# Two-layer transformer on one core: the middle stage's last batch written tile by tile, with banks and key buffers of its own

## The reference, cut to what matters

```
attn   = softmax(q k^T / 4) v                      # 16 heads of 16
out    = (sigmoid(gate) * mem_out / denom + (1 - sigmoid(gate)) * attn) @ Wo.T
x      = out + experts of layer 0 ; xn = layernorm(x)
q1, k1 = silu(xn @ Wq1), silu(xn @ Wk1) ; v1 = silu(xn @ Wv1)
sg     = sigmoid((xn @ Wg1) @ Wg2)                 # Wg1: 256 x 16
logits = xn @ router1                              # 256 x 8, top 2, softmax over the two
```

## Time and profile before

| what | us |
|---|---|
| median of 3 runs | 997.73 (994.32 to 1004.47) |
| the profiled execution | 995.28 |
| its span in the profile | 993.4 |
| busy: TensorE, VectorE, ScalarE, GpSimd | 837.8, 573.7, 394.2, 311.4 |
| middle stage's last outT copied | 567.31 |
| first transfer of the next stage | 635.38 |

### The profile page before, as it was taken

The page is one execution under the profiler, slowest core; times in us unless marked ns, Lnnn a source line. Parts: engine busy times, 40 slices in busy tenths (PEclk is TensorE's granted clock), DMA queues, the critical chain, the costliest instruction groups (busy, mean ns, idle before and its releaser), DMA issues. The chain is left out here.

```text
span 993.4 us, 14867 instructions
## 1 busy us (share of the span) xinstructions
PE 837.8 (84%) x4544; PEld 486.6 (49%) x4544; DVE 573.7 (58%) x1269; ACT 394.2 (40%) x676; POOL 311.4 (31%) x250
## 2 busy tenths in 40 slices
PE   4989999848998987997988748399799999999990
PEld 4765655501223443433434436256566666666660
DVE  7746877258779776777674435424343443444435
ACT  2336666414555565466446604022122222222220
POOL 3033567363001330151015113214243344344230
PEclk9999999956999997999798966599899999999995
DMA  8514655463222323533403301799773344344007
GB/s 273 136 59 146 198 184 183 151 187 92 86 67 61 117 85 100 170 106 107 145 27 107 127 21 61 213 288 307 209 171 99 92 125 115 90 116 124 23 16 259
DMA packets 158353, 130.26 MB, mean 131 GB/s; under 512 B 64128, under 2 KB 139920, under 8 KB 158288
## 3 DMA queue, kind: packets, MB, share of 16 engines
q1 hardware_dynamic: 151136, 109.89, 37.6%
q0 software_dynamic: 7152, 19.54, 6.7%
HBM read 83.37 MB, written 46.01 MB: 130 GB/s over the span
## 5 line engine op out<-in xcount | busy, mean ns | idle before, releaser
L1305 DVE TENSOR_REDUCE b_negmax<-b_psM 128x1 f32<-128x512 f32 x256 | 163.0, 683 | 61.0 <-PE b_psM L1491 58.2
L1242 ACT ACTIVATE b_probs<-b_psE 128x512 f32<-128x512 f32 x256 | 138.8, 594 | 125.9 <-PE b_psE L1509 125.1
L1491 PE MATMUL b_psM<-b_kst,b_qst 96*128 96x512 bf16 x256 | 98.5, 427 | 42.1 <-DVE b_negmax L1305 26.0
L1509 PE MATMUL b_psE<-b_qst,b_kst 98*128 98x512 bf16 x256 | 87.9, 405 | 14.1 <-ACT b_probs L1242 9.6
L2007 PE MATMUL d_psG<-d_w,d_xT 128*128 x156 | 76.9, 616 | 2.5 <-issue 1.4
L1860 POOL DMA_INDIRECT scratch_ys<-d_y,put x39 | 39.7, 1018 | 122.4 <-ACT d_y L1891 120.8
L2032 PE MATMUL d_psY<-d_w,d_hidden 128*128 x312 | 76.8, 390 | 0.8 <-ACT d_hidden L1885 0.8
L2015 PE MATMUL d_psU<-d_w,d_xT 128*128 x156 | 75.0, 603 | 0.0
L1491 PEld LDWEIGHTS b_psM<-b_kst,b_qst 96*128 96x128 bf16 x256 | 24.5, 99 | 101.4 <-DVE b_negmax L1305 76.7
L1518 PE MATMUL b_psV<-b_probs,b_vst 128*32 128x512 f32 x512 | 71.9, 634 | 2.5 <-ACT b_probs L1242 2.5
L1509 PEld LDWEIGHTS b_psE<-b_qst,b_kst 98*128 98x128 bf16 x256 | 20.4, 98 | 101.0 <-issue 51.8
(11 more groups left out here) (353 smaller groups left out, 1591.0 us busy)
## 6 DMA issues: line engine op xcount, KB each, us to landing
scratch_parts<-a_parts SPq DMA_DIRECT2D x12, 512.0 KB, 4.2
b_qst<-scratch_parts SPq DMA_DIRECT2D x96, 64.0 KB, 2.1
b_kst<-scratch_parts SPq DMA_DIRECT2D x96, 64.0 KB, 2.1
scratch_parts<-b_part SPq DMA_DIRECT2D x24, 256.0 KB, 3.1
d_qst<-scratch_parts SPq DMA_DIRECT2D x96, 64.0 KB
d_kst<-scratch_parts SPq DMA_DIRECT2D x96, 64.0 KB
scratch_ys<-a_y SPq DMA_DIRECT2D x39, 128.0 KB, 1.8
scratch_v<-a_xn SPq DMA_DIRECT2D x4, 1024.0 KB, 6.9
```

Source lines behind the costliest of these rows:

```text
L1242: nc.scalar.activation(probs[k % PSLOTS][:, h, :], psE[h % 2][:, :], ACT.Exp, scale=float(HD) ** -0.5).then_inc(scores_used[h % 2], 1)
L1305: nc.vector.tensor_reduce(negmax[i][:, t, h:h + 1], psM[:, h % 2, :], AX_X, ALU.max, negate=True).then_inc(rows_used[h % 2], 1)
L1491: nc.tensor.matmul(psM[:, h % 2, :], qst[g][0:STACK, h, t * P:(t + 1) * P], kst[g][0:STACK, h, :], start=True, stop=True).then_inc(rows_re ...
L1509: nc.tensor.matmul(psE[h % 2][:, :], kst[g][0:STACKM, h, k * P:(k + 1) * P], qst[g][0:STACKM, h, :], start=True, stop=True).then_inc(score ...
```

## The change

For the last batch the shared steps are replaced by a function `finish` on each engine.

- The V projection of the third batch is no longer in slot 15 of the fourth batch's attention; it comes in `finish`, behind the output projection.
- Heads, turn and output projection, residual, moments, the turn of xn and its split go by tile, in psM, psV and the banks of the scores (psS, the old psE in one tensor).
- The last batch's k has buffers of its own (half1, parts1, in the memory of probs). Its parts are made by ScalarE and GpSimd; the last one was made on VectorE.
- The order on TensorE is: small projection, q with the logits' turn between its halves, k, rank, turn of k, V, gate, inversion.
- On VectorE the tables follow the choice at once, the decayed k comes behind the ids, the weights of the two experts come last. The gate and the exponential of the weights are last on ScalarE.

For all batches the small projection is made with its result turned: the weights (24 columns) stand still and the 512 rows pass, in 6 products. VectorE copies the 24 x 512 result (lowT), and four small products with the identity turn logits and gate input (24 columns for each tile). The choice of experts moves from slot 10 to 11, its exponential on ScalarE from 11 to 12, and its weights from 12 to 13.

TensorE's order between the last scores and the norm, before. psV<-b_probs is `values`, b_outT and b_qf are the heads, b_combined the turn, b_wo the output projection; the rows b_wv ahead are the end of the 24 of V.

The three instructions on b_part are gone from VectorE, and the decayed k stands behind the ids. The diff, cut to its core:

```diff
-            for slot in sorted(steps):
...
+            finish(BATCHES - 1)
+
+        def final(b, g, k):
+            return isinstance(b, int) and b == BATCHES - 1 and g == GROUPS - 1 and k == TILES - 1
+
+        half1 = probs[1][:, 0:KT, :]
+        parts1 = [probs[0][:, j, :].bitcast(BF16).rearrange("p (k t) -> p k t", k=KT) for j in range(3)]
+        turned = [psM[:, 0, 0:KT * P], psM[:, 1, 0:KT * P], psS[:, 0, 0:KT * P], psS[:, 1, 0:KT * P]]
+        projected = [psV[:, 0:D], psM[:, 0, 0:D], psV[:, 0:D], psS[:, 0, 0:D]]
...
+            def finish(n):
+                store(n - 1)
+                store_xn(n)
+                sp.wait_ge(qd_done, n + 1)
+                sp.dma_start(scratch["qd"][n].rearrange("k p n -> p k n"), qd[:, :, :]).then_inc(stored, 16)
+                store_parts(n, 0, parts)
+                sp.wait_ge(kd_done, n + 1)
+                sp.dma_start(scratch["kd"][n].rearrange("(t p) n -> p t n", p=P), kd[:, :, :]).then_inc(stored, 16)
+                sp.wait_ge(v_done, n + 1)
+                sp.dma_start(scratch["v1"][n].rearrange("(t p) n -> p t n", p=P),
+                             v32[:, :, :, :].rearrange("p t h w -> p t (h w)")).then_inc(stored, 16)
+                store_parts(n, 1, parts1)
+                store_gate(n)
...
+            def finish(n):
+                for t in range(TILES):
+                    combine(t)(n)
+                power(n)
+                decay_q(n)
+                rest(0)(n)
+                third(n)
+                pool.wait_ge(part_done[0], 2 * n + 2)
+                pool.wait_ge(k_ps, n + 1)
+                nc.gpsimd.tensor_tensor(half1, half1, parts1[0], ALU.subtract).then_inc(rest_done, 1)
+                pool.wait_ge(part_done[1], 2 * n + 2)
+                nc.gpsimd.tensor_tensor(parts1[2], half1, parts1[1], ALU.subtract).then_inc(part_done[2], 1)
...
+            def finish(n):
+                for t in range(TILES):
+                    act.wait_ge(combT_ps, n + t + 1)
+                    nc.scalar.activation(combT[:, :, t * P:(t + 1) * P], psX[:, t % 2, 0:KT * P].rearrange("p (k n) -> p k n", k=KT),
+                                         ACT.Copy).then_inc(combT_done, 1)
+                silu_v(n - 1)
+                for t in range(TILES):
+                    act.wait_ge(xT_ps, n + t + 1)
...
+                silu_half(0)(n)
+                first_part(n)
+                act.wait_ge(half_ps, 2 * n + 2)
+                nc.scalar.activation(half1, psM[:, :, :], ACT.Silu).then_inc(half_done, 1)
+                second_part(n)
+                act.wait_ge(half_done, 2 * n + 2)
+                nc.scalar.activation(parts1[0], half1, ACT.Copy).then_inc(part_done[0], 1)
+                act.wait_ge(v_ps, n + 1)
+                act.wait_ge(stored, STORES * n)
+                nc.scalar.activation(v32[:, :, :, 0:HD], psM[:, :, :].rearrange("p a (t h d) -> p (a t) h d", t=2, d=HD),
+                                     ACT.Silu).then_inc(v_done, 1)
+                act.wait_ge(rest_done, 2 * n + 2)
+                nc.scalar.activation(parts1[1], half1, ACT.Copy).then_inc(part_done[1], 1)
+                gate(n)
+                gap_exp(n)
...
+            loop(act, attend, {4: (copy_combT,), 8: (copy_xT,), 9: (silu_half(0),), 10: (first_part,), 11: (second_part,),
+                               12: (silu_half(1), gap_exp), 14: (gate,), 15: (silu_v,)}, finish)
...
-            def copy_low(n):
-                small = second(n)[:, 0, 0:TILES * RW].rearrange("p (t n) -> p t n", n=RW)
+            def copy_lowT(n):
                 dve.wait_ge(low_ps, n + 1)
-                nc.vector.tensor_copy(low[:, :, :], small[:, :, E:RW]).then_inc(low_done, 1)
-                routing.choose_pair(dve, n, small[:, :, 0:E], hot)
-
-            def copy_lowT(n):
-                dve.wait_ge(lowT_ps, n + 1)
-                nc.vector.tensor_copy(lowT[:, :], second(n)[0:HD, 1, :]).then_inc(lowT_done, 1)
+                nc.vector.tensor_copy(lowT[:, :], psX[0:RW, 0, :]).then_inc(lowT_done, 1)
+
+            def choose(n):
+                dve.wait_ge(logits_ps, n + 1)
+                small = psX[:, 1, 0:TILES * RW].rearrange("p (t n) -> p t n", n=RW)
+                routing.choose_pair(dve, n, small[:, :, HD:RW], hot)
...
+            def finish(n):
+                for t in range(TILES):
+                    weigh_terms(t, psS if t % 2 else psM)(n)
+                for t in range(TILES):
+                    dve.wait_ge(y_ps, n + t + 1)
+                    dve.wait_ge(y0_added, 4 * n + 4)
+                    x = norm.rows(xacc, n, t)
+                    nc.vector.tensor_tensor(x, projected[t], x, ALU.add).then_inc(residual_done, 1)
+                    dve.wait_ge(residual_done, n + t + 1)
+                    norm.moment(n, t, xacc)
+                norm.gather_moments(dve, n)
+                dispatch.prepare(dve)
+                norm.apply(dve, n, xacc, xn)
+                for t in range(TILES):
+                    dve.wait_ge(xhi, n + t + 1)
...
+                dve.wait_ge(low_ps, n + 1)
+                nc.vector.tensor_copy(lowT[:, :], psV[0:RW, :]).then_inc(lowT_done, 1)
+                dve.wait_ge(logits_ps, n + 1)
+                routing.choose_pair(dve, n, psE[1][:, 0:TILES * RW].rearrange("p (t n) -> p t n", n=RW)[:, :, HD:RW], hot)
+                dve.wait_ge(routing.chosen, 2 * BATCHES)
+                dispatch.pick(dve)
+                dispatch.positions(dve)
+                dispatch.spread_ids(dve)
+                decay_k(n)
+                dispatch.spread_rows(dve)
+                dispatch.owners(dve)
+                dispatch.tables(dve)
+                route_weights(n)
...
+            loop(dve, attend, {0: (weigh_terms(0),), 1: (weigh_terms(1),), 2: (weigh_terms(2),), 3: (weigh_terms(3),), 5: (residual,),
+                               6: (moments,), 7: (normalise, find_next), 8: (split_xT,), 10: (copy_lowT, fold_next(0)),
+                               11: (choose, fold_next(1)), 12: (fold_next(2),), 13: (decay_k, first_part, route_weights, fold_next(3)),
+                               14: (second_part,), 15: (third_part,)}, finish, ready)
...
-            def logits_low(n):
-                if not alone(n):
-                    pe.wait_ge(half_done, 2 * n + 1)
+            def project_low(n):
+                pe.wait_ge(half_done, 2 * n + 1)
+                mm = three(nc, psX[0:RW, 0, :], [(wr[0][:, k, :], wr[1][:, k, :], xT[0][:, k, :], xT[1][:, k, :])
+                                                       for k in range(KT)])
+                mm.then_inc(low_ps, 1)
+
+            def turn_logits(n):
+                pe.wait_ge(lowT_done, n + 1)
                 for t in range(TILES):
-                    c = slice(t * P, (t + 1) * P)
-                    mm = three(nc, second(n)[:, 0, t * RW:(t + 1) * RW],
-                               [(xT[0][:, k, c], xT[1][:, k, c], wr[0][:, k, :], wr[1][:, k, :]) for k in range(KT)])
-                mm.then_inc(low_ps, 1)
-
-            def turn_low(n):
-                pe.wait_ge(low_done, n + 1)
-                for t in range(TILES):
...
-                mm.then_inc(lowT_ps, 1)
+                    mm = nc.tensor.matmul(psX[:, 1, t * RW:(t + 1) * RW], lowT[:, t * P:(t + 1) * P], ident[0:RW, 0:RW],
+                                          start=True, stop=True, skip_group_check=True)
+                mm.then_inc(logits_ps, 1)
...
+            def finish(n):
+                def turn_combined(t):
+                    pe.wait_ge(combined_done, TILES * n + t + 1)
+                    if t < 2:
+                        pe.wait_ge(gate_done, n)
+                    else:
+                        pe.wait_ge(combT_done, n + t - 1)
+                    for k in range(KT):
+                        mm = nc.tensor.transpose(psX[:, t % 2, k * P:(k + 1) * P], combined[:, t, k * P:(k + 1) * P], ident[:, :])
+                    mm.then_inc(combT_ps, 1)
+
+                def project_out(t):
+                    pe.wait_ge(combT_done, n + t + 1)
+                    if t == 2:
+                        pe.wait_ge(residual_done, n + 1)
+                    elif t:
+                        pe.wait_ge(terms, TILES * n + t + (2 if t == 1 else 1))
+                    for k in range(KT):
+                        mm = nc.tensor.matmul(projected[t], combT[:, k, t * P:(t + 1) * P], wo[:, k, :],
+                                              start=k == 0, stop=k == KT - 1, skip_group_check=True)
+                    mm.then_inc(y_ps, 1)
+
...
+
+                pe.wait_ge(out_copied, GROUPS * (n + 1))
+                pe.wait_ge(qf_in, 16 * n + 16)
+                for used in rows_used:
+                    pe.wait_ge(used, 2 * TILES * GROUPS * BATCHES)
+                spread_heads(psM, n, 0)
+                for used in scores_used:
+                    pe.wait_ge(used, 2 * TILES * GROUPS * BATCHES)
+                spread_heads(psS, n, 1)
+                turn_combined(0)
```

(44 more changed lines are left out.)

153 lines of the change are left out of this document (68 added, 85 removed).

## The result

The changed kernel takes 971.37 us (median of 4 runs, 969.58 to 975.94), the kernel before 1000.54 beside it (4 runs, 994.32 to 1004.47). The ratio is 0.9743, with a 95% interval from 0.970 to 0.9786. The forecast was 977.5 in a range from 967 to 989, faster: right in sign and range, 6 us too high. As a gain it was further off: 18.1 us were forecast from the profiled execution, and the profiled executions span 993.4 us before and 967.7 after. The 25.7 us between them are what has to be explained.

The account below looks back on a forecast made before the run. The last batch's 68.07 us tail, one chain through TensorE, VectorE, ScalarE and GpSimd, was taken as uncovered. Loop 3.7, handover 2.6 and tail 11.8 make 18.1 off 995.28: 977.2, stated as 977.5, range 967 to 989.

Parts of the forecast that it names:

- Loop: Batches 0 to 2: six 512-column products replace 24 small ones, scores come earlier; 3.7 us gained, ends 0 and 6.
- rival 3: VectorE sets the loop: choice behind slot 11's reductions delays the next rows; loop gain 0 or −2, 981 to 983; chance 0.07.
- Handover: Last exponentials to outT's copy: V's 24 products move behind the output projection, values() starts earlier; 2.6 us gained.
- my lower case: In the handover, values() at 1.2 GHz takes 2 us, against 1.1 at 2.4 GHz.
- Tail: outT's last copy to the next stage's first transfer: T+56.3 against T+68.07, 11.8 us gained.
- Behind the rank: Rank's end R to next stage's start: R+26.3, between R+25 and R+27; 23.55 us before.
- Upper clock through the tail: Upper clock holds through the tail: R at T+26, end at T+52.3, gain 22.1, total 973; chance 0.13.
- VectorE in the loop: VectorE sets the loop, its choice delaying the next rows: loop gain 0 or −2, 981 to 983; chance 0.07.
- Lower clock: Tail at the lower clock with GpSimd and VectorE meetings costing 5 to 8: gain 7 to 11, 984 to 988; chance 0.17.
- no shrinking: Tail does not shrink because of a missed wait: T+61 to 66, little from the loop, 986 to 992; chance 0.10.
- last stage's clock: Unchanged last stage starts in another clock state; below grant 0.89 it eats the 18 us, at 0.86 1006; chance 0.03.
- Rival 2: Lower clock and the port in the tail: R at T+41, end at T+63.4 to 67.3, 984 to 988; chance 0.17.

Follow-up runs that it names:

- the kernel in which TensorE stood 1.1 us for the SiLU: Changed kernel with the last batch's keys' two products waiting again for the queries' SiLU: 975.07 us, ratio 0.979.
- the addition's move: Changed kernel with one of VectorE's four additions of the first layer's rows moved from slot 11 to slot 12: 973.73 us, ratio 0.9739.

## Why the prediction was right, and by how much it was off

- **Loop, 3.7 us: measured 6.6.** The direct saving was priced about right: the products are 1.2 us shorter in iterations 1 and 2 and 1.9 in iteration 3, and ScalarE's wait behind them shrank by 1.2, 1.2 and 2.1 us, where the earlier trace rows, my source, shows only the last and slowest. Where it would arrive was wrong. In iterations 1 and 2 the third group, in which the 24 products stood, gave nothing, since VectorE's choice in slot 11 set it: one half of rival 3 was true. But TensorE got 1.6 us further ahead there, and that paid out in the next group, and in the last batch's groups too; with the small projection alone it is 7.2 us. How much of this the change makes is not settled: by the kernel before profiled again, some 4.7 us of it was clock luck, and 2.7 of luck went against it.
- **Handover, 2.6 us: measured 2.1.** Right; values() ran at 1.2 GHz, my lower case, with 0.14 us of waiting.
- **Tail, 11.8 us: measured 14.6.** xT was split at T+18.3 (19.5 foretold), R came at T+27.2 (30). The difference of 2.8 us is put down to the clock: I had let the lower level in on both sides of the split. The runs show it on one at most. When the part up to the split ran at 0.83 to 0.85, the part to R was at 1.00 and took 8.9 us; when it ran at 0.88 to 0.91, it was 0.8 us shorter and the part to R 1.6 longer, but for the kernel in which TensorE stood 1.1 us for the SiLU, where both were fast. In all kernels with this order of products, V ahead or not, R came between T+27.1 and T+28.1. What decides between the two was not tried.
- **Behind the rank, 26.3 us: measured 26.19.** Both parts of it hold: GpSimd's hold on VectorE 7 us foretold, 6.76 measured by taking it away; and the gate's chain last, shown by freeing it (its store issued at R+20.0, R+21 foretold; the next stage 6.15 us behind it, 6.05 foretold). The Trainium skill (SBUF — State Buffer, "Who interferes with whom") names instructions with two SBUF inputs and, in their two-port modes, copies, casts and tensor-scalars as those that contend with GpSimd; reductions, it says, never do on this chip. By that rule the trace agrees: the four stalled instructions are a cast, two tensor-scalars and the scan, which has two SBUF inputs though its name is not in the list, and the reductions ran at their usual 0.29 and 0.42 us beside GpSimd.
- **Left out:** 1.0 us before the middle and 1.3 in the last stage, both unchanged code. With them 6.6 + 2.1 + 14.6 + 1.0 + 1.3 = 25.6 of the 25.7 us. Unchanged code gave its 2.3 us by luck, which brought the total further from the forecast, not nearer.
- **The rivals.** Upper clock through the tail: half true, from the split to the rank but not ahead of it (0.84), and its 973 is the nearest of all to the 971.37 measured. VectorE in the loop: true of its place, false of its price. Lower clock, no shrinking, last stage's clock: not seen (0.95 granted there). Rival 2's sum has a slip: with stalls of 5 to 8 us in place of the 7 in R+26.3, and R at T+41, the end is at T+65.3 to 68.3, not T+63.4 to 67.3.

Open: what in the tile-by-tile order gives its 9.8 us up to the split, since no run undid heads, projections or norm by themselves; what decides between the clock's two patterns in the tail; the 6.4 us in which no engine held VectorE on one chip, and why the addition's move kept nothing even with the stores early (last groups 25.7 and 25.5 us on that chip against 24.7 and 23.9).

## What to carry to other kernels

Where stages of work are walked in slots, price a shorter operation by what the next group gets, not by its own slot: an engine that gets ahead is paid at the next place where it was the last. A long chain of tiny VectorE instructions should not run beside GpSimd passes over whole tiles: each pass that it met here cost the chain the rest of that pass, and starting the chain 1.3 us earlier just moved it under another pass. And look for waits that both kernels share: moving one line of stores by two slots took 6.2 us off two groups and 4.2 off the time to the next stage, the whole rewritten tail 14.6.

## What the runs showed of the hardware

- A TENSOR_TENSOR_SCAN of 8 elements took 0.17 us alone and 1.92 beside a GpSimd subtraction, ending 0.03 us after it. A cast of 32 elements: 0.18 and 1.55.
- GpSimd was hardly slowed by this: its subtractions took 2.12 to 2.25 us in all profiles, 2.76 where a VectorE instruction with two bf16 tiles as inputs (1.49 us) still had 0.78 us to run, and 3.31 in the kernel before, where the same one had 1.33 to run. In these meetings the instruction that was under way first was not held up.
- Unchanged code took different times between chips: an iteration's third group in the kernel before 23.3 us in one profile and 32.4 on another chip, and its median 993 to 1013 us. In the changed kernels that group took 22.3 to 23.3 us in all profiles but the two of that chip (27.6 to 28.1). Only ratios against a kernel run on the same chip compare.
- The 24 products of 24 columns took 2.93 us at 2.4 GHz and 5.49 at 1.2; the six of 512 columns that replace them 1.73 at 2.4.
